# A transformer block on one core: weighting placed behind the second score phase, taps that lag a step, x loaded once in place, weight sums in halves

## What is computed

```python
def bit_linear(x, w):                      # act_quant: per token, 127 levels
    return einsum('bsd,hd->bsh', act_quant(x), weight_quant(w))
def attention(q, k, v, Wq, Wk, Wv, Wo):    # softmax over 128 keys, 16 heads
    ...
def ffn(x, w1, conv_w, conv_b, w2):
    h = bit_linear(x, w1)
    h = depthwise_conv1d(h) + conv_b       # 3 taps along s, per channel
    return bit_linear(silu(h), w2)
x = x + tanh(g_xattn) * attention(layernorm(x), ctx, ctx, ...)
x = x + tanh(g_ffn) * ffn(layernorm(x), ...)
```

## Time and profile before

| what | us |
|---|---|
| median of 3 runs | 286.36 |
| profiled execution | 285.66 |
| its span, first to last instruction | 283.9 |
| TensorE matmuls busy | 219.6 (77%) |
| VectorE busy | 200.8 (71%) |
| ScalarE busy | 148.1 (52%) |
| POOL busy | 133.8 (47%) |

### The profile page before, as it was taken

How to read it: one execution, slowest core, us unless ns; L and a number is a source line. 1 busy time by engine, 2 the same in 40 slices (tenths; PEclk the granted TensorE clock), 3 DMA queues, 4 the chain that set the end, 5 groups by cost and what they waited for, 6 DMA issues and landing times.

```text
span 283.9 us, 6533 instructions
## 1 busy us (share of the span) xinstructions
PE 219.6 (77%) x2408; PEld 177.7 (63%) x2424; DVE 200.8 (71%) x406; ACT 148.1 (52%) x264; POOL 133.8 (47%) x233
## 2 busy tenths in 40 slices
PE   0696779987988789889889899888756856764773
PEld 0675657766867678678768777766634644553663
DVE  0305134788687588988988988978569969998672
ACT  1040816445446366675675684674845446565350
POOL 3202020623623438568567676546485646554331
PEclk9997959999999999999999999999997979999799
DMA  6938110100101101001001000000000100110111
GB/s 206 320 79 268 37 28 11 38 22 21 38 4 38 29 12 39 18 21 39 20 21 25 29 9 2 0 3 2 0 1 2 37 18 21 37 37 22 37 39 57
DMA packets 11553, 11.97 MB, mean 42 GB/s; under 512 B 1026, under 2 KB 11266, under 8 KB 11522
## 3 DMA queue, kind: packets, MB, share of 16 engines
q1 hardware_dynamic: 11522, 11.55, 13.0%
HBM read 9.45 MB, written 2.10 MB: 41 GB/s over the span
## 4 chain that ended last, share of the span: by engine, by line
PE 42%; DVE 20%; issue 17%; ACT 9%; POOL 8%; DMA 1%; SPq 1%; POOLq 0%; DVEq 0%; ACTq 0%
DVE smax L782 9%; PE ps_proj L366 6%; PE ps_av L417 6%; PE ps_proj L358 5%; PE ps_score L393 5%; PE ps_score L374 4%; POOL hid L293 3%; DVE y L838 3%; PE ps_max L403 3%; ACT y L656 3%; PE ps_av L427 2%; PE ps_av L522 2%; POOL zdeq L305 2%; PE ps_av L570 2%; PE ps_h L470 2%
## 5 line engine op out<-in xcount | busy, mean ns | idle before, releaser
L782 DVE TENSOR_REDUCE smax<-ps_max 128x8 f32<-128x1024 f32 x32 | 39.1, 1222 | 25.4 <-PE ps_max L403 25.4
L630 ACT ACTIVATE prob<-ps_score 128x1024 f32<-128x1024 f32 x32 | 32.8, 1024 | 21.0 <-PE ps_score L393 20.5
L393 PE MATMUL ps_score<-Qs,KT 32*128 32x128 f32 x512 | 37.1, 282 | 4.2 <-DVE smax L782 2.3
L403 PE MATMUL ps_max<-KT,QT 32*128 32x256 f32 x256 | 36.3, 400 | 1.5 <-DVE smax L782 1.5
L393 PEld LDWEIGHTS ps_score<-Qs,KT 32*128 32x128 f32 x512 | 31.4, 186 | 9.3 <-issue 8.4
L270 POOL TENSOR_SCALAR var<-mv 128x1 f32<-128x1 f32 x16 | 3.9, 244 | 64.0 <-DVE mv L813 63.9
L838 DVE SCALAR_TENSOR_TENSOR y<-hid,conv,y 128x508 f32<-128x508 f32 x32 | 29.3, 915 | 6.2 <-ACT y L656 5.8
L656 ACT ACTIVATE y<-hid,conv 128x512 f32<-128x512 f32 x32 | 25.8, 814 | 14.6 <-DVE hid L831 9.4
L570 PE MATMUL ps_av<-w2q,zqT 128*128 128x256 f16 x128 | 18.7, 294 | 12.2 <-DVE xres L936 11.4
L841 DVE SCALAR_TENSOR_TENSOR y<-hid,conv,y 128x508 f32<-128x508 f32 x32 | 24.7, 773 | 1.1
L570 PEld LDWEIGHTS ps_av<-w2q,zqT 128*128 128x128 f16 x128 | 12.3, 105 | 19.9 <-DVE xres L936 17.3
(11 more groups left out here) (110 smaller groups left out, 543.3 us busy)
## 6 DMA issues: line engine op xcount, KB each, us to landing
xin<-x SPq DMA_DIRECT2D x16, 128.0 KB, 2.1
cin<-ctxT SPq DMA_DIRECT2D x16, 128.0 KB, 2.0
xres<-x SPq DMA_DIRECT2D x1, 2048.0 KB, 8.5
out<-xres SPq DMA_DIRECT2D x16, 128.0 KB, 1.7
w1f<-w1T SPq DMA_DIRECT2D x1, 1024.0 KB, 7.3
w2f<-w2T SPq DMA_DIRECT2D x1, 1024.0 KB, 9.1
wk<-wkT SPq DMA_DIRECT2D x1, 256.0 KB, 3.6
wv<-wvT SPq DMA_DIRECT2D x1, 256.0 KB, 3.9
```

The source lines that it names most:

```text
L393: mm = pe.matmul(ps_score[:, i * 512 + j * P:i * 512 + (j + 1) * P], KT[b % 3][rows, j * P:(j + 1) * P], Qs[rows, j * P:(j + 1) * P], star ...
L403: mm = pe.matmul(ps_max[:, i * 512 + t * 2 * P:i * 512 + (t + 1) * 2 * P], QT[n % 2][rows, t * P:(t + 1) * P], KT[n % 3][rows, t * 2 * P:( ...
L630: act.activation(prob[pair][:, :], ps_score[:, :], ACT.Exp, scale=DH ** -0.5).then_inc(exp_done, 1)
L782: dve.tensor_reduce(dst, ps_max[:, :].rearrange("p (g t e k) -> p g t e k", g=PG, t=KD, e=2), AX.X, ALU.max).then_inc(max_done, 1)
```

## The change

TensorE's step begins with the output projection of sequence d (one step later than before, into the queries' PSUM instead of the weighted sums'), weighting, x transposes; then come maxima and weighted-sum transposes, projections, and the integer transposes directly ahead of the hidden tile. The transposes of x wait for the first residual of d. Middle taps move from their own step to the next, as do the outer taps. In a step POOL rounds before it scales the even tile. From tile 20 on VectorE scales all tiles, and POOL's quantisation of block v in the late loop waits until the outer taps of round v - 2 are done. x is loaded once, straight to xres, with a semaphore for each sequence; the context has four buffers. The load order starts with context 0, the key weights and x 0. The warm-up has 10 products and waits for the fp32 identity alone; keys and values of sequence 0 are projected ahead of its first transposes. VectorE makes masks and constants ahead of the first statistics. The absolute sums are made in halves, w1's in step 0 and w2's in step 1, with the mean behind step 1 instead of ahead of it. A dummy SiLU loads its table early.

```diff
-WARM = 14
+WARM = 10
...
-        ps_o = ps_av[:, 0:D]
+        ps_o = ps_q
...
             def load_x(i):
-                wait(sp, xn_done, i - 1)
-                sp.dma_start(xin[i % 2][:, :], x[i * P:(i + 1) * P, :]).then_inc(x_in[i % 2], 16)
+                sp.dma_start(xres[:, i * D:(i + 1) * D], x[i * P:(i + 1) * P, :]).then_inc(x_in[i], 16)
 
             def load_c(i):
-                wait(sp, v_ready, i - 1)
-                sp.dma_start(cin[i % 2][:, :], ctxT[i * P:(i + 1) * P, :]).then_inc(c_in[i % 2], 16)
+                wait(sp, v_ready, i - CB + 1)
+                sp.dma_start(cin[i % CB][:, :], ctxT[i * P:(i + 1) * P, :]).then_inc(c_in[i % CB], 16)
...
-            load_x(0)
             load_c(0)
             load_w(wk, wkT, KD, wk_in)
+            load_x(0)
             load_w(wv, wvT, KD, wv_in)
             load_w(wq, wqT, KD, wq_in)
             load_x(1)
             load_c(1)
             sp.dma_start(gate_row[:, :], gates).then_inc(gate_in, 16)
+            load_x(2)
+            load_c(2)
             load_w(w1f, w1T, KD, w1_in)
-            load_x(2)
+            load_x(3)
+            load_c(3)
             load_w(w2f, w2T, NC_, w2_in)
             load_w(wo, woT, KD, wo_in)
-            load_c(2)
-            load_x(3)
             sp.dma_start(conv[:, :], cwb).then_inc(small_in, 16)
-            sp.dma_start(xres[:, :].rearrange("p (b n) -> p b n", b=NB),
-                         x.rearrange("(b p) n -> p b n", p=P)).then_inc(xres_in, 16)
-            load_c(3)
             for i in range(4, NB):
...
             def quantise2(v):
                 gp.wait_ge(zs_done, v + 1)
+                if v - 2 in LATE:
+
+                    gp.wait_ge(conv_done, LATE[v - 2][-1])
...
-                for T in TILES.get(s, ())[0:1]:
-                    dequantise(T)
                 if seq(s - 2):
                     round1(s - 2)
+                for T in TILES.get(s, ()):
+                    if on_gp(T):
+                        dequantise(T)
...
-            dequantise(20)
...
-                for T in LATE.get(v - 2, ()):
-                    if T % 2 == 0:
-                        dequantise(T)
...
-                wait(pe, aT_done, n - 2)
+                wait(pe, x1_done, n - 2)
...
-                wait(pe, x1_done, a)
+                wait(pe, att_done, a)
...
             def step(s):
                 b, n, a, d = s, s + 1, s - 1, s - 2
                 tiles = TILES.get(s, ())
-                if seq(b):
-                    max_transpose(b)
-                if seq(d - 1):
-                    int_transpose(d - 1, min(tiles, default=0))
-                if seq(n):
-                    project_v(n)
+                if seq(d):
+                    project_out(d)
                 if seq(a):
                     weigh(a)
                 if seq(n):
+                    x_transpose(n)
+                if seq(b):
+                    max_transpose(b)
+                if seq(a):
+                    unweighted_transpose(a)
+                if seq(n):
+                    project_v(n)
                     project_q(n)
+                if seq(d - 1):
+                    int_transpose(d - 1, min(tiles, default=0))
                 for T in tiles[0:1]:
                     hidden(T, s - 2)
-                if seq(a):
-                    unweighted_transpose(a)
                 row_stage(b, 0)
                 for T in tiles[1:2]:
                     hidden(T, s - 2)
...
                 if s == NB - 1:
                     y_transpose(0)
                 row_stage(b, 1)
-                if seq(a):
-                    project_out(a)
-                if seq(n + 1):
-                    x_transpose(n + 1)
 
...
-            pe.wait_ge(ident16_done, 1)
             for i in range(WARM):
                 pe.matmul(ps_av[:, 0:P], ident[:, :], ident[:, :], start=True, stop=True)
-            x_transpose(0)
             pe.wait_ge(wk_in, 16)
             project_k(0)
             pe.wait_ge(wv_in, 16)
             project_v(0)
+            x_transpose(0)
             pe.wait_ge(wq_in, 16)
             project_q(0)
             project_k(1)
             row_stage(-1, 0)
             row_stage(-1, 1)
-            x_transpose(1)
             pe.wait_ge(v_ones, 2)
             step(0)
             pe.wait_ge(gate_in, 16)
-            pe.wait_ge(mask_done, 1)
-            pe.matmul(ps_setup[:, 0:2], ones[0:1, :], gate_row[:, :], start=True, stop=True)
-            pe.wait_ge(abs_done, 1)
-            pe.matmul(ps_setup[:, 2:4], ones[:, :], abs_sum[:, :], start=True, stop=True).then_inc(sums_ready, 1)
-            pe.wait_ge(wo_in, 16)
+            pe.wait_ge(ones_done, 1)
+            pe.matmul(ps_setup[:, 0:2], ones[0:1, :], gate_row[:, :], start=True, stop=True).then_inc(gate_ready, 1)
             step(1)
             pe.wait_ge(gate_done, 1)
+            pe.wait_ge(abs_done, 1)
+            for half in range(2):
+                mm = pe.matmul(ps_setup[:, 2:4], ones[:, :], abs_sum[:, 2 * half:2 * half + 2],
+                               start=(half == 0), stop=(half == 1))
+            mm.then_inc(sums_ready, 1)
+            pe.wait_ge(wo_in, 16)
             pe.wait_ge(mean_done, 1)
+            pe.wait_ge(ident16_done, 1)
             for s in range(2, SB + 2):
...
+            project_out(NB - 2)
+            weigh(NB - 1)
             int_transpose(NB - 3, 20)
-            weigh(NB - 1)
             hidden(20, NB - 2)
...
+                last = TILES.get(s - 1, ())
                 if seq(a):
                     exponent(a, 1)
-                if seq(d - 1):
-                    int_copy(d - 1)
-                if seq(n):
-                    x_copy(n)
+                for T in last[0:1]:
+                    middle_tap(T)
+                extra(0)
                 if seq(a):
                     u_copy(a)
                 if seq(n):
+                    x_copy(n)
+                extra(1)
+                for T in last[1:2]:
+                    middle_tap(T)
+                if seq(n):
                     v_copy(n)
                     q_copy(n)
+                if seq(d - 1):
+                    int_copy(d - 1)
                 if 0 in tiles:
                     w2_sums_copy()
                 for T in tiles[0:1]:
                     raw_copy(T)
-                extra(0)
                 exponent(b, 0)
                 if seq(a):
                     att_copy(a)
-                for T in tiles[0:1]:
-                    middle_tap(T)
                 if seq(n + 1):
                     k_copy(n + 1)
-                for T in tiles[1:2]:
-                    middle_tap(T)
-                extra(1)
...
+            step(0, weight_sums(0))
+            act.wait_ge(gate_ready, 1)
             act.activation(gate[:, :], ps_setup[:, 0:2], ACT.Tanh).then_inc(gate_done, 1)
-            for s in range(1, SB + 2):
+            step(1, weight_sums(1))
...
+            middle_tap(18)
             exponent(NB - 1, 1)
+
+            act.activation(scratch[:, :], ones[:, 0:1], ACT.Silu)
+            act.wait_ge(w2q_done, PIECES)
             act.wait_ge(w1q_done, PIECES)
-            act.wait_ge(w2q_done, PIECES)
+            u_copy(NB - 1)
             silu(0)
             int_copy(NB - 3)
-            u_copy(NB - 1)
-            raw_copy(20)
+            middle_tap(19)
+            att_copy(NB - 1)
             silu(1)
             middle_tap(20)
-            att_copy(NB - 1)
             quantised_copy(0)
...
-                for T in before[-1:]:
+                for T in last[0:1]:
                     outer_taps(T)
+                if seq(a):
+                    normalise(a)
                 if seq(d):
                     quantise1(d)
-                if seq(a):
-                    normalise(a)
                 if seq(n):
                     row_max(n, 1)
                 for T in tiles[1:2]:
                     dequantise(T)
+                for T in last[1:2]:
+                    outer_taps(T)
                 extra(0)
                 extra(1)
-                if s < NB - 1:
-                    for T in tiles[:-1]:
-                        outer_taps(T)
...
             residual1(NB - 2)
             outer_taps(18)
+            normalise(NB - 1)
             token_scale(0)
-            normalise(NB - 1)
+            dequantise(20)
+            outer_taps(19)
             quantise1(NB - 2)
-            outer_taps(19)
             residual1(NB - 1)
+            token_scale(1)
             dequantise(21)
-            token_scale(1)
             outer_taps(20)
             quantise1(NB - 1)
...
                     outer_taps(T - 1)
-                    if T % 2:
-                        dequantise(T)
+                    dequantise(T)
```

126 lines of the change are left out of this document (65 added, 61 removed).

## The result

The changed kernel takes 276.99 us (median of 5 runs, 274.05 to 277.66) against 286.36 us (5 runs beside it, 284.3 to 286.93): a ratio of 0.966, 95% interval 0.9615 to 0.9705. The prediction was 275.5 us, with a range of 268 to 283. It was the fastest of the five, 2.9 us under the median, where the profiled execution before stood 0.7 under its own: the traces differ by 11.6 us, the medians by 9.4.

A forecast was written before the change was run, and what follows sets the result against it. In the steps, the loop between nearly full TensorE and VectorE bounds; in the head, nothing is full. -11.5 - 2.6 + 3.6 + 3.0 - 3.1 = -10.6 from 285.66 or 286.36 us: said 275.5, range 268 to 283.

The forecast's parts named there:

- Head: From the start to the maxima of step 2: 11.5 us less, bounds -13.2 and -7.
- copy of x transposed: In the head, this copy stands behind two key copies on ScalarE, adding 1.0 us ahead of step 0's maxima.
- the half-clock stretch that I gave back: Between the maxima of steps 0 and 2: TensorE still stands between first maxima, so one slow stretch costs 1.7 us.
- Steps 2 to 5: Steps with the ternary pieces on VectorE: 10.24 us each against 10.9, together 2.6 us less.
- the loop that I had described: In steps 2 to 5, the transposes of x wait for the first residual, at R + 1.66 us.
- Steps 6 to 15: Steps with tiles, with a new stall of 0.90 us each: a step of 11.3, together +3.6, bounds +2.3 and +11.
- my first sum: TensorE's path through a step of 6 to 15, stall included: 9.83 + 0.30 + 0.16 + 0.89 = 11.18 us.
- R: Delay of pair 0's maxima behind the end of TensorE's second score phase: 1.41 us in steps 2 to 5, then 0.58.
- My second floor: In steps 6 to 15, a second lower bound on the step: R + 10.40 us, with R = 0.58 under the first.
- the rival "no stall": Steps with tiles lack the 0.90 us stall at the hidden tile: steps near 10.4, 7.2 less, 268 us; chance 10%.
- The rival "lock": POOL's dequantisation holds VectorE's outer tap every step with tiles: step 12.25, 7.6 us more, 283 us; chance 11%.
- Hand-over and late loop: Step 15 to the late loop: +3.0 us, bounds 0 and +5; then the late loop: -3.1, bounds -5 and +3.

The follow-up runs named there:

- e11: Changed kernel with VectorE's old start order, both statistics first, and the warm-up waiting for the bf16 identity: 283.38 us, ratio 0.9887.
- e9: Changed kernel with the absolute sums whole, both in step 0, and the mean ahead of step 1: 280.97 us, ratio 0.982.
- e2: Changed kernel with a one-column copy as first activation, ahead of ScalarE's first wait: 275.06 us, ratio 0.9591.
- e4: Changed kernel with POOL scaling the step's even tile before it rounds: 274.17 us, ratio 0.9599.
- e1: Changed kernel with the integer transposes earlier, behind the maxima's transposes, and their copies ahead of the values' copy: 277.52 us, ratio 0.9701.
- e6: Changed kernel with the edits of e1 and e4 together: 269.17 us, ratio 0.943.
- e8: Changed kernel with the edits of e1, e4 and e2, and the last exponent ahead of the middle tap of tile 18: 268.38 us, ratio 0.9391.
- e12: Changed kernel with the edits of e1, e4 and e2, hand-over as in the changed kernel: 266.89 us, ratio 0.9298.
- e3: Changed kernel without the wait of POOL's late-loop quantisation for the outer taps: 281.31 us, ratio 0.9829.
- e10: Kernel before the change with only the late-loop wait of POOL's quantisation for the outer tap added: 288.17 us against 285.79, ratio 1.0083.
- e0: The changed kernel run again, unedited, beside the first three experiments: 275.56 us, ratio 0.9644.
- e7: Changed kernel with the old warm-up length, 28 passes (14 products instead of 10): 276.32 us, ratio 0.9663.

## Why the prediction was right, term by term

**Head: the cause is right, 1.3 us too much expected.** The early warm-up carries it (e11), and the halves add to it (e9), though what each is worth depends on the other. The term that was mis-sized is the 1.0 added for the "copy of x transposed" behind "two key copies on ScalarE". Before, the copy of x was the first activation, with its table load at 0.72, in idle time. Now the first activation is a key copy, and the load stands behind its waits, at 8.14 for 1.28 us, with keys and values already projected. e2 shows it: without it 15.50, as predicted. From step 0's maxima to step 2's I had 19.5 + 1.7 = 21.2, and it took 21.3; the half-clock stretch that I gave back is there (granted 0.55 from 16.70 to 24.00, the 1.2 GHz level for nearly all of it). This agreement is partly luck. The step that holds the stretch took 10.63 (16.73 to 27.36) where I had 7.85 + 1.7 = 9.55, and step 1 with sums and mean took 10.64 (to 38.00) where I had 11.65.

**Steps 2 to 5: right in kind, half the gain.** Settled steps took 10.47 (from the maxima at 45.08 to those at 55.55) where the sum had 10.24. It had no wait in it for the copy of the queries. Two rows of TensorE in step 3, after:

```profile
50.61 0.41 PE L352 MATMUL ps_proj<-ident,xn 128*128 128x128 f32 x2 [0.70 <-DVE xres L821]
...
54.33 0.38 PE L402 MATMUL ps_score<-Qs,KT 32*128 32x128 f32 x2 [0.28 <-ACT QT L636]
```

The wait on the residual is the loop that I had described. The 0.28 is what I took to be covered. The rest of the miss is in step 2: I credited it with 0.5 and it took 10.86 where it had taken 10.75, probably because its first maxima start right behind TensorE's phase, so that the loop first fills up to its delay; no run isolates that.

**Steps 6 to 15: the mechanism right, the account of it half right.** The stall "between the pair back to back" is there at the size that I had: 154.06 - 152.77 = 1.29 from start to start, less 0.39 of work, is 0.90 (the 0.73 of the row counts from the modelled end of the matmul). Weighting waits 0.16 where I had 0.30, the transposes of the weighted sums not at all where I had 0.16, and the transposes of x wait 0.26 for the residual, which my first sum did not have: 9.83 + 0.16 + 0.26 + 0.89 = 11.14, the measured step. The lock costs the tap up to 0.31, within my 0.2 to 0.4. The remaining miss of this stage is at its ends: the last of these steps took 10.83, and the 0.67 that I had added for a later R did not come.

What failed is the price of removing the stall. My second floor, R + 10.40 with R = 0.58, is 10.98, and 11.3 with the lock that I took; R without a lock is 0.59 in e4 (161.91 less 161.32), as I had it. Both floors hold the stall of 0.89, so the rival "no stall" took it off both, with the lock unchanged: 7.2 us. e1 removed the stall and a settled step gained nothing, since POOL's L302 then starts 0.20 ahead of the tap and the lock grows from 0.30 to 0.87. With the lock away and the stall kept (e4) the step is 11.05. Only with both away (e6) does it fall to 10.26. The rival "lock" was wrong the same way: its 12.25 took the whole 1.27 in each step, and where the lock is at its fullest (e1) it adds 0.87 to the tap and the step is 11.13.

The rule that I cited from the Trainium skill, page "SBUF — State Buffer", section "Who interferes with whom", is borne out in its kind: the tap, with two SBUF inputs, takes 1.62 beside POOL's product in e1 and 0.74 behind it in e4. The whole 1.27 that it allows was not reached.

**Hand-over and late loop: right in the totals.** +2.7 for +3.0. The order of waits is the one walked, the last weighting 1.14 behind TensorE's previous work and the normalisation 3.92 behind VectorE's:

```profile
192.08 1.08 PE L426 MATMUL ps_av<-prob,V 128*32 128x128 f32 x32 [1.14 <-ACT prob L641]
...
197.49 0.26 DVE L813 RECIPROCAL rden<-ps_av 128x16 f32<-128x16 f32 x1 [3.92 <-PE ps_av L436]
```

But e8 shows that the last exponent's place does not set the total, so that step of the walk was not needed for it. I had walked it at full clock, and it was not: granted 0.50 from 201 to 211 us, where the old hand-over had 0.98 over its whole length. With the same order the other kernels take from 27.0 (e12, granted 0.94) to 30.8 us (e1, granted 0.78), so 2.7 for 3.0 is good fortune within that spread.

The late loop gave -3.0 for -3.1. One locked tap is priced to 0.01 us (e3), but I counted nine of 1.43 from one row. The old loop had five of 1.43 and four of 1.25, one of the four being

```profile
258.09 1.25 DVE L838 SCALAR_TENSOR_TENSOR y<-hid,conv,y 128x508 f32<-128x508 f32 x1
```

which makes 5 x 0.68 + 4 x 0.50 = 5.4 instead of 6.1, and -2.4 with the five even tiles. VectorE's busy time fell by 2.5 (41.0 to 38.4), and the rest came out of its waits, which I had not priced. The coupling that e10 shows I had not seen.

**Drain: missed, -1.3.** I had "unchanged". One product of it, after:

```profile
252.90 1.09 PE L523 MATMUL ps_max<-ident,y 128*128 128x128 f32 x8 [1.12 <-DVE y L855]
254.81 1.05 PE L580 MATMUL ps_av<-w2q,zqT 128*128 128x256 f16 x8 [0.82 <-DVE xres L948]
```

and before:

```profile
263.19 1.09 PE L515 MATMUL ps_max<-ident,y 128*128 128x128 f32 x8 [3.54 <-DVE y L841]
265.11 1.89 PE L570 MATMUL ps_av<-w2q,zqT 128*128 128x256 f16 x8 [0.82 <-DVE xres L936]
```

The same eight products took 1.89, after a wait of 3.54 ahead of the transposes, and take 1.05, after one of 1.12: the old drain began at the lower clock level (granted 0.66 from 263 to 268 us), the new one at the upper (1.00 from 253 to 258). The shorter wait looks like the cause, but the other kernels do not bear that out. e4, e6 and e12 have the late loop of the changed kernel, at the 42.2 us that it takes in e0, and their drains take 20.1, 20.1 and 21.7 us at a granted 0.92, 0.92 and 0.84, where e0's takes 19.5 at 0.97. What decides where the clock falls stays open, and with it how much of the -1.3 is the change's.

Two errors (the head too good by 1.3, the drain too bad by 1.3) cancel, and so, with steps 2 to 5 too good by 1.3 and steps 6 to 15 too bad by 2.0, do the two kinds of steps. The closeness of 275.5 to 276.99 is partly that, and partly the choice of execution: by the traces I forecast 1.0 us too little gain, by the medians 1.2 too much (10.6 against 11.6 and 9.4).

Of my signs, the maxima of step 0 (16.73), the stall (0.73) and the first taps of the late loop (none above 0.75) came as said. Step 2 at 38.00 was not near 36, the step of 11.14 and the rounds of 3.95 lie just under what I gave, and one sign of being wrong was there as well: the clock was at 0.50 until 23 us, beyond my 20.

## What to carry to other kernels

Before pricing the removal of a stall, walk every loop that passes through the step, with the locks at the places where the new order puts them: two loops of 11.1 us hid each other here, each edit alone was worth 0.0 and 0.1 us in a settled step, and both together were worth 6 us. When a start is reordered, look at what becomes the first activation and how many waits stand ahead of it; here a one-column activation at the top of the list hid the table load. A wait that avoids a conflict is paid by everything queued behind it on the same engine, so move that work away first. Where two changes lie on one path, as the early start and the halves do, what each seems to be worth depends on which is taken out, and the two figures do not add up.

## What the hardware showed that was not expected

In ScalarE's list the table load stands directly ahead of the first activation, but not always behind what that activation waits for. In the changed kernel four waits stand ahead of the key copy (the masks, the ones beside the values, the key and the value projection), and the load of 1.28 us starts at 8.14, behind the last of them. In the kernel before one wait stood ahead of the copy of x, and in e2 one ahead of the one-column copy, and there the load starts at 0.72:

```profile
0.72 1.28 ACT L602 ACT_TABLE_LOAD   x1 [0.72 <-PEq L988]
15.85 0.38 ACT L602 ACTIVATE xnT<-ps_proj 128x256 f32<-128x256 f32 x1 [13.85 <-PE ps_proj L343]
```

So the copy of x waited until 15.85 while its load was long done. Whether it is the number of waits that decides is not shown by a run. The Trainium skill, page "ScalarE: Activation LUTs", says in its section "Step-by-step: what each stage is for" that the compiler places the load right before the activation that needs it. The trace agrees on the order, and adds that waits ahead of that activation can hold the load too.

By the length of its passes the warm-up itself ran at the lower clock level, although the profile's clock column reads 1.00 there. Its 20 passes of 128x128 took 4.43 us (1.63 to 6.06), 0.22 each, and the 28 of the kernel before 0.21 each, where passes of the same size in a settled step take 0.11 (eight for the queries in 0.89, 151.88 to 152.77).

TensorE's granted clock falls in the head of every kernel of this study, though it is busy there 4.0 of 5 us: 0.67 from 15 to 20 us in e2, 0.55 from 16.70 to 24.00 after. Ahead of it, from 6.60 to 16.70, TensorE was busy 5.96 of 10.10 us at a granted 0.99. A gain of 1.2 us at step 0 (e2) was 0.3 at step 2, with a second such stretch in between. The same code does not always get the same clock: e1 and e4 run the changed kernel's head and fall to 0.67 already from 10 to 15 us. Which pattern of work keeps the clock up was not found: a warm-up longer by 8 passes (e7) does not.
